# Exponentials of an attention kernel written to four SBUF buffers instead of back to PSUM, and the scaling of the row sums moved from VectorE to ScalarE

## The reference

```python
qkv = (x @ w_qkv.T).reshape(B, S, 3 * H, D)          # S = 1024, H = 16 heads, D = 128
logits = jnp.einsum('bqhd,bkhd->bhqk', q, k) * scale
weights = jax.nn.softmax(logits, axis=-1)
combined = jnp.einsum('bhqk,bkhd->bqhd', weights, v).reshape(B, S, H * D)
return combined @ w_out.T
```

## Time and profile before

| what | value |
|---|---|
| runs | 938.49 us median of 3 (938.06 to 946.85) |
| the profiled execution | 939.58 us, its span in the profile 937.8 us |
| PE, DVE, ACT, POOL busy over the span | 88%, 83%, 69%, 46% |
| first attention with preparation | about 0 to 594 us |

### The profile page before, as it was taken

The page is one execution under the profiler, slowest core; times in us unless marked ns, Lnnn a source line. Parts: engine busy times, 40 slices in busy tenths (PEclk is TensorE's granted clock), DMA queues, the critical chain, the costliest instruction groups (busy, mean ns, idle before and its releaser), DMA issues.

```text
span 937.8 us, 13391 instructions
## 1 busy us (share of the span) xinstructions
PE 827.9 (88%) x4330; PEld 471.9 (50%) x4330; DVE 775.4 (83%) x1605; ACT 646.5 (69%) x1170; POOL 427.3 (46%) x439
## 2 busy tenths in 40 slices
PE   2799989999999989988989998589878999998997
PEld 1344444454455454454445454367655555554686
DVE  2689999899989999999999998575689686885637
ACT  3588868887888777777877878454555757667631
POOL 3124354444454357777778673161322434443301
PEclk9999999999999999999999999799989999999999
DMA  3288757967778677776865677330000000000001
GB/s 121 35 160 191 154 97 156 193 115 146 174 142 153 131 136 143 149 128 135 161 124 108 127 137 142 60 104 1 1 1 1 1 0 2 0 2 1 1 1 45
DMA packets 276870, 86.32 MB, mean 92 GB/s; under 512 B 267584, under 2 KB 272448, under 8 KB 276416
## 3 DMA queue, kind: packets, MB, share of 16 engines
q1 hardware_dynamic: 275520, 80.05, 44.5%
q0 software_dynamic: 992, 5.34, 1.8%
q10 hardware_dynamic: 288, 0.07, 0.0%
HBM read 17.29 MB, written 1.05 MB: 20 GB/s over the span
## 4 chain that ended last, share of the span: by engine, by line
DVE 39%; PE 30%; issue 14%; ACT 12%; DMA 3%; POOL 2%; SPq 1%; POOLq 0%; ACTq 0%; DVEq 0%
DVE nmax L1746 9%; DVE EP L1761 8%; DVE ptm L1864 4%; PE ps L1094 4%; PE ps L1117 4%; PE ps L1096 4%; PE ps L1095 4%; PE ps L1355 3%; PE ps L1341 3%; PE ps L1132 3%; PE ps L1320 3%; DVE ps L1950 2%; ACT ps L1513 2%; DVE ql L1728 2%; DVE st L1661 1%
## 5 line engine op out<-in xcount | busy, mean ns | idle before, releaser
L1523 ACT ACTIVATE EP<-ps,rinv 128x1024 f16<-128x1024 f32 x128 | 142.6, 1114 | 42.0 <-DVE rinv L1756 41.5
L1761 DVE SCALAR_TENSOR_TENSOR EP<-ps,rinv,EP 128x1024 f16<-128x1024 f32 x128 | 163.2, 1276 | 5.3 <-ACT EP L1523 5.1
L1746 DVE TENSOR_REDUCE nmax<-ps 128x1 f32<-128x1024 f32 x128 | 155.7, 1217 | 0.6 <-PE ps L1096 0.6
L1513 ACT ACTIVATE ps<-ps,nms,s_unit 128x1024 f32<-128x1024 f32 x128 | 150.7, 1177 | 4.3
L1094 PE MATMUL ps<-kh,qh 128*128 128x512 f16 x256 | 98.3, 384 | 26.6 <-DVE EP L1761 24.5
L2101 POOL TENSOR_TENSOR wgu<-wgu,ptm 128x688 f32<-128x688 f32 x60 | 100.4, 1673 | 42.4 <-DVE ptm L1864 40.4
L1094 PE MATMUL ps<-ET,VH 128*128 128x512 f16 x256 | 98.3, 384 | 16.2 <-DMA ET<-EP 9.6
L1095 PE MATMUL ps<-ET,VH 128*128 128x512 f16 x256 | 98.3, 384 | 0.0
L1096 PE MATMUL ps<-ET,VL 128*128 128x512 f16 x256 | 98.0, 383 | 0.0
L1095 PE MATMUL ps<-kl,qh 128*128 128x512 f16 x256 | 97.5, 381 | 0.0
L1096 PE MATMUL ps<-kh,ql 128*128 128x512 f16 x256 | 97.5, 381 | 0.0
(11 more groups left out here) (251 smaller groups left out, 2132.5 us busy)
## 6 DMA issues: line engine op xcount, KB each, us to landing
wqr<-in_wqk SPq DMA_DIRECT2D x16, 256.0 KB, 3.7
wgu<-in_tern POOLq DMA_DIRECT2D x3, 1024.0 KB, 6.3
wvr<-in_wv SPq DMA_DIRECT2D x8, 256.0 KB, 4.2
wor<-in_wo SPq DMA_DIRECT2D x16, 128.0 KB, 3.4
ET<-EP SPq DMA_TRANSPOSE x128, 4.3
X<-in_x SPq DMA_DIRECT2D x2, 512.0 KB, 5.7
prw<-in_down_idx POOLq DMA_DIRECT2D x2, 256.0 KB, 6.4
tern<-in_l_wuq_rep SPq DMA_DIRECT2D x1, 512.0 KB, 4.9
```

The costliest lines, as they stand in the source:

```text
L1513: e.activation(bank, bank, ACT.Exp, bias=nms[:, c:c + 1], scale=s_unit[:, h4:h4 + 1], accum_out=rsum[:, c:c + 1]).then_inc(exped.sem, 1)
L1523: e.mul(EP[:, n % NE_RING, 0, :], SB(u, j), rinv[:, c:c + 1]).then_inc(e_hi.sem, 1)
L1746: e.tensor_reduce(nmax[:, c:c + 1], SB(u, j), AX.X, ALU.max, negate=True).then_inc(maxed.sem, 1)
L1761: e.scalar_tensor_tensor(out=EP[:, n % NE_RING, 1, :], in0=SB(u, j), scalar=rinv[:, c:c + 1], in1=EP[:, n % NE_RING, 0, :], op0=ALU.mult, ...
```

## The change

The exponentials go to a new SBUF tensor `E32` of four tiles, one for each tile of a unit. Its place in SBUF is that of `XH` and `XL`, which are first used when the attention is over. The high half and the low half are formed from `E32`. The PSUM pair is therefore released by the exponential (`exped`) and no longer by `rest_e`. An exponential now waits until the low half of the same tile one unit earlier is done. The scaling of the row sum becomes a step of its own, r, which ACT issues directly behind each exponential; DVE keeps the reciprocal.

```diff
-    order = ("i3 f0 F0 A7 M0 S0 h3 p0 e0 l3 X0 x0 o0 i0 h0 e1 O0 y0 x1 S1 M1 l0 S2 X1 p1 w0 w1 p4 S3 i1 y1 A0 "
+    order = ("r3 i3 f0 F0 A7 M0 S0 h3 p0 e0 r0 l3 X0 x0 o0 i0 h0 e1 r1 O0 y0 x1 S1 M1 l0 S2 X1 p1 w0 w1 p4 S3 i1 y1 A0 "
...
+        with ExitStack() as ctx:
+            E32 = sbuf(ctx, "E32", [P, 4, 1024])
         XH = sbuf(top, "XH", [P, 2, 1024], F32R)
         XL = sbuf(top, "XL", [P, 2, 1024], F32R)
...
-                free_scores[i] = e_lo[at]
+                free_scores[i] = exped[at]
...
-                    e.activation(bank, bank, ACT.Exp, bias=nms[:, c:c + 1], scale=s_unit[:, h4:h4 + 1],
+                    if u >= 1:
+                        w.wait_ge(*e_lo[u - 1, j])
+                    e.activation(E32[:, j, :], bank, ACT.Exp, bias=nms[:, c:c + 1], scale=s_unit[:, h4:h4 + 1],
                                  accum_out=rsum[:, c:c + 1]).then_inc(exped.sem, 1)
+                elif what == "scale_sum":
+                    u, j = at
+                    c = 4 * (u % 2) + j
+                    w.wait_ge(*exped[u, j])
+                    if u >= 2:
+                        w.wait_ge(*inverted[u - 2, j])
+                    e.mul(rsc[:, c:c + 1], rsum[:, c:c + 1], 1.0 / E_UP).then_inc(sum_down.sem, 1)
...
-                    e.mul(EP[:, n % NE_RING, 0, :], SB(u, j),
+                    e.mul(EP[:, n % NE_RING, 0, :], E32[:, j, :],
                           rinv[:, c:c + 1]).then_inc(e_hi.sem, 1)
...
-                    w.wait_ge(*exped[u, j])
                     if u >= 2:
                         w.wait_ge(*e_lo[u - 2, j])
-                    e.tensor_scalar(rsc[:, c:c + 1], rsum[:, c:c + 1], 1.0 / E_UP, None, ALU.mult).then_inc(sum_down.sem, 1)
                     w.wait_ge(*sum_down[u, j])
                     e.reciprocal(rinv[:, c:c + 1], rsc[:, c:c + 1]).then_inc(inverted.sem, 1)
...
-                    e.scalar_tensor_tensor(out=EP[:, n % NE_RING, 1, :], in0=SB(u, j),
+                    e.scalar_tensor_tensor(out=EP[:, n % NE_RING, 1, :], in0=E32[:, j, :],
                                            scalar=rinv[:, c:c + 1], in1=EP[:, n % NE_RING, 0, :], op0=ALU.mult,
                                            op1=ALU.subtract).then_inc(e_lo.sem, 1)
```

More of the change, by code:

```diff
@@ L134, in order_of_heads @@
     before = ("t0 t1 n0 n1 n2 n3 n4 k0 T0 K0 Q0 v0 n5 n6 n7 X0 x0 y0 T1 X1 y1 X2 y2 x1 Q1 x2 x3 v1 v2 S0 X3 M0 "
-             "e0 y3 S1 x4 e1 v3 h0 v4 X4 e2 x5 M1 y4 S2 i0 l0 M2 i1 h1 i2 M3 X5 S3 y5 l1 x6 l2 X6 h2 x7 X7 e3 "
+             "e0 r0 y3 S1 x4 e1 r1 v3 h0 v4 X4 e2 r2 x5 M1 y4 S2 i0 l0 M2 i1 h1 i2 M3 X5 S3 y5 l1 x6 l2 X6 h2 x7 X7 e3 "
              "y6 y7").split()
@@ L159, in order_of_heads @@
         else:
-            todo.append(({"S": "scores", "M": "max", "e": "exp", "i": "row_inv", "h": "cast_e", "l": "rest_e"}[what], 0, j))
+            todo.append(({"S": "scores", "M": "max", "e": "exp", "r": "scale_sum", "i": "row_inv", "h": "cast_e", "l": "rest_e"}[what], 0, j))
     todo += [("load_wv", 2), ("split_wo", 0), ("load_wo", 1), ("square_wv", 2)]
     loads = []
-    order = ("i3 f0 F0 A7 M0 S0 h3 p0 e0 l3 X0 x0 o0 i0 h0 e1 O0 y0 x1 S1 M1 l0 S2 X1 p1 w0 w1 p4 S3 i1 y1 A0 "
-             "A1 X2 A2 M2 p2 l1 i2 M3 y2 h1 e2 x2 A3 A4 A5 A6 h2 l2 w2 p3 e3").split()
-    last = ("f0 o0 w3 i3 A7 O0 L0 h3 l3 L1 F0 L2 L3 A0 L4 A1 A2 A3 w5 A4 L5 L6 L7 A5 A6 w4").split()
+    order = ("r3 i3 f0 F0 A7 M0 S0 h3 p0 e0 r0 l3 X0 x0 o0 i0 h0 e1 r1 O0 y0 x1 S1 M1 l0 S2 X1 p1 w0 w1 p4 S3 i1 y1 A0 "
+             "A1 X2 A2 M2 p2 l1 i2 M3 y2 h1 e2 r2 x2 A3 A4 A5 A6 h2 l2 w2 p3 e3").split()
+    last = ("f0 o0 w3 r3 i3 A7 O0 L0 h3 l3 L1 F0 L2 L3 A0 L4 A1 A2 A3 w5 A4 L5 L6 L7 A5 A6 w4").split()
     end = ("F0 o0 A7 U0 f0 O0 O1 U1 o1").split()
@@ L196, in order_of_heads @@
                 todo.append(({"S": "scores", "M": "max", "e": "exp"}[what], u + 1, j))
-            elif what in "ihl":
-                todo.append(({"i": "row_inv", "h": "cast_e", "l": "rest_e"}[what], u if j == 3 else u + 1, j))
+            elif what in "rihl":
+                todo.append(({"r": "scale_sum", "i": "row_inv", "h": "cast_e", "l": "rest_e"}[what], u if j == 3 else u + 1, j))
             elif what == "A" and j < NA:
@@ L538, in build @@
         qkv_lo, maxed, e_lo, o_lo, inverted = (signal(n, "DVE") for n in ("qkv_lo", "maxed", "e_lo", "o_lo", "inverted"))
-        o_added, sum_down = signal("o_added", "DVE"), signal("sum_down", "DVE")
+        o_added, sum_down = signal("o_added", "DVE"), signal("sum_down", "ACT")
         abs_summed, all_summed = signal("abs_summed", "ACT"), signal("all_summed", "PE")
@@ L697, in build @@
                 exped.mark(*at)
+            elif what == "scale_sum":
+                sum_down.mark(*at)
             elif what == "row_inv":
-                sum_down.mark(*at)
                 inverted.mark(*at)
```

## The result

The changed kernel takes 963.59 us (median of 4, 963.31 to 964.71), the kernel before 938.83 us (median of 4 runs beside it). The ratio is 1.0246, 95% interval 1.019 to 1.0302: slower by 2 to 3%, 25 us. The profiled execution took 964.71 us with a span of 963.0 us, 25.2 us more than the one before.

A forecast was written before the change was run, and what follows sets the result against it. DVE was taken to bound the attention from 300 us on, sharing the chain with PE before. Terms 2 + 7 + 14 + 6 + 4 + 5 - 2 gave + 36 us, forecast 974 us, range 946 to 1006.

The forecast's parts named there:

- The low half reads SBUF twice: DVE's low half in the attention, both tensors in SBUF, waits out any running POOL instruction, 0.8 us each, 55 us in all.
- the lower bound of 25: Low halves' total wait if they start mostly behind POOL's instructions: 25 us, leaving + 8 with the small terms.
- the first rival: DVE and POOL are in step, so low halves miss POOL's instructions and the kernel gets faster, 921 us; chance 0.08.
- POOL as the bound of 400 to 500 us: In that stretch POOL's work, low halves and DVE's look-ups exclude each other, 115 us in 100: + 14 us.
- The look-ups on DVE meet POOL more often: POOL's work is pushed out of the low halves' time into the rest, so DVE's look-ups wait more: + 5 us.
- The scaling leaves DVE: Without the row sum's scaling DVE saves 0.18 us for each of 128 tiles in the attention, 23 us.
- ACT gets 128 small instructions: The scaling adds 37 us to ACT, 85% busy and not the bound; later row sums and near misses cost + 4.
- The pair's earlier release: PE gets back part of its wait for the score pair: - 3 us at 60 to 300 us, - 2 in the last stretch.
- The dodge: Low halves miss POOL's instructions because DVE and POOL are in step; DVE's saving then gives 921 us; chance 0.08.
- ACT's latency: Rival: the chain from exponential to low half gets 0.3 us longer per tile, DVE stands before the reciprocal, 976 us; chance 0.07.
- three signs by which the prediction would be wrong: Low half's line stays at 1275 ns, DVE stands before the reciprocal, or the attention ends before 594 us.
- Half the rate: Rival: two SBUF sources without bf16 halve the low half's throughput, 1.19 us more each, about 1120 us; chance 0.02.

## Why the prediction was right, and where its terms were wrong

The forecast was 974 us, + 36 on the profiled execution; measured were 963.6 and + 25. The direction and the mechanism of the largest term were right. Its size was not, nor was the place in time, nor what ACT's instruction costs, and the total lies in the range partly by luck.

- *The low half reads SBUF twice.* Right as a mechanism, shown by the run in which that operand alone changed: 17 to 18 us. Its size was wrong. The prediction multiplied POOL's busy share by 0.8 us and got 55 us of waits; the changed profile has 22.9, near the lower bound of 25. The price of one wait was right, 0.81 us. How many wait was wrong: 28 low halves waited, where the product of the shares has some 68. Two things took the rest away. POOL was at work at 52 of the 123 starts behind 60 us, 42%, where its share of the time is 61%; this is the first rival's argument, and it held in part. And of these 52 only 28 waited, 17 of the other 24 because they met POOL's own term of the look-up, which holds DVE up only in its first part (0.63 us of 2.58). "Waits for the whole of the other" is true of the additions and false of this instruction. The forecast mean of 1.7 us was 1.45.
- *The stretches.* Forecast were + 2 us for 60 to 300 us, + 7, + 14 and + 6 for the next three. By the starts of the low halves the attention lost 14 us by 300 us, then 2, 2 and 4. The low halves' own waits were 3.5, 5.8, 7.5 and 6.0 us there, against 19.8, 11.2, 13.4 and 10.3. The first stretch is where DVE's standing time grew most, from 18.8 to 30.5 us, and where the stall near 75 us lies, which no term had.
- *POOL as the bound of 400 to 500 us, + 14.* It did not come to that. POOL's busy time there was 80.7 of 100 us with its own waits inside, and DVE was busy for 96.5.
- *The look-ups on DVE meet POOL more often, + 5.* They did not: their busy time fell from 57.9 to 52.3 us.
- *The scaling leaves DVE, - 23* (of which the sum counts 17, half of the first stretch left out). Wrong in its effect. The instructions went, but the run without any scaling gained 13 us: DVE is the bound in part of the attention only, and what it gains elsewhere it stands away.
- *ACT gets 128 small instructions, + 4, "ACT does not become the bound by its load".* This step failed. The load is only 26 us, but in program order it stands ahead of copies that DVE waits for. It costs 8 us without any reader and 15 with one. A queue that the prediction itself put at 85% busy was taken for one with room.
- *The pair's earlier release, - 5 in two stretches.* No gain: PE's wait for the low half is gone from the list and reappears as waits for the transposes (21.2 us after, 9.6 before, in the whole span) and for DVE's other lines. That DVE would be late anyway was right.
- *The rivals.* The dodge was partly true in the size, as said. ACT's latency had a chance of 0.07 as the sole cause. One of the three signs by which the prediction would be wrong did appear: DVE stood before the reciprocal, 18.3 us in place of 7.4. ACT's part is half of what DVE newly lost (22 of 45 us), but set against the time that the move saves it is a small part of the net 25 us: the SBUF buffers alone cost 19. The prediction had no case in which both act. Half the rate is excluded by the shortest and the median low half, 1267 and 1276 ns.

So the total was right within its range because two errors have opposite signs. In the sum of + 36 the move of the scaling stands for about - 13 (- 17 and + 4) and all the rest for + 49. Measured were + 2 us for the move made alone and + 19 for the SBUF buffers made alone: 15 us too little for the one and 30 too much for the other.

## What to carry to other kernels

Moving an operand of a DVE instruction from PSUM to SBUF can cost more than the PSUM bank it frees: look first whether the instruction then has two tensors in SBUF while POOL works there. In the trace the sign is a line whose shortest and median stay and whose longest grows. Ask also which instruction of POOL is met: the additions held DVE up nearly to their end, the term of the look-up only for its first quarter. And moving a small instruction to a less busy engine was not free here, because copies that others wait for stand behind it in that engine's program order; a constant that absorbs it was worth 1.5%.

What one change costs depends on what else holds the path. On top of the SBUF buffers, moving the scaling cost about 3 us while POOL's look-up ran (1.0246 against 1.0208, inside the intervals), and 9 to 11 us with the look-up cut (1.003 against 0.9915, clear of them).

## What the runs showed of the hardware

A gap in PE's work within the attention was followed by a lower clock. In the changed kernel, PE at 75 to 85 us (in the kernel before it was busy for 4.49 and 5.00 us there, at a granted clock of 1.00):

```profile
75.00:80.00 5.00, 1.27 (x5) 0.81 0.93 190
80.00:85.00 5.00, 5.00 (x20) 0.51 0.57 108
```

After a stretch with 1.27 us of work in 5, in which PE stood 3.73 us for a transpose, the granted clock was 0.51 for the next 5 us, its lower level of 1.2 GHz. Products of 512 columns followed each other at 0.43 us there and at 0.21 us from 85 us on. The stall came from one transpose that stood for 7.41 us in the chain of waits:

```profile
71.44 7.41 DMA ET<-EP
78.85 0.25 issue
79.09 0.59 PE ps L1098
79.68 0.43 PE ps L1099
```

ACT is a little slower with SBUF in PSUM's place. The groups of its two large lines in the kernel before were:

```profile
L1523 ACT ACTIVATE EP<-ps,rinv 128x1024 f16<-128x1024 f32 x128 | 142.6, 1114 | 42.0 <-DVE rinv L1756 41.5
...
L1513 ACT ACTIVATE ps<-ps,nms,s_unit 128x1024 f32<-128x1024 f32 x128 | 150.7, 1177 | 4.3
```

The exponential, which now writes SBUF, took 1204 ns in place of 1177, and the high half, which now reads SBUF, 1144 in place of 1114. The Trainium skill ("ScalarE: Activation LUTs", section "Step-by-step: what each stage is for") says that ScalarE writes PSUM faster than SBUF; the trace agrees, by 27 ns for 1024 columns. A small ACT instruction whose factor is a number took 203 ns, one whose factor is read from a tile 294.
